# Rounding constants of a block quantisation in two PSUM banks, copied to SBUF by ScalarE for GpSimd's subtraction

## Chip, cores and metric

One core of a Trainium2 chip runs the whole program. The metric is the device time of one execution in microseconds, lower is better. The engines are named as in the profile: PE (TensorE), DVE (the Vector engine), ACT (ScalarE), POOL (GpSimd) and SP (SyncE, which only issues DMAs here).

## What is computed

Two transformer-like layers over x of shape (4, 1024, 256). Each branch is: layer norm with a modulation of scale and shift, the branch, a gated residual. Layer 0 has a dilated causal attention and a linear layer whose input and weight are quantised. Layer 1 has a Mamba block (a convolution, a selective state-space scan over time with 512 channels and 16 states) and a gated recurrence. What matters here is the quantisation of layer 0 and, as the load beside it, the scan of layer 1.

```python
def _mx_quantize(t, eps=1e-30):            # blocks of 32 along the features
    scales = max(max|block| / 7.5, eps)
    q = nearest value of the FP6 grid (2 exponent bits, 3 mantissa bits) to block / scale
...
xd = (xq * xs[..., None]).reshape(x2.shape)
out = xd @ wd.T + bias
...
def step(h, inp):                          # Mamba: one step in time
    h = a * h + bx
    y = einsum('bds,bs->bd', h, c)
```

The grid is reached by rounding in floating point. For a scaled value v the exponent bits of v are kept (a bitwise and with 0x7F800000), the result is raised to at least 1 and multiplied by 1.5 * 2^20. Adding this constant to v and subtracting it again rounds v to 3 mantissa bits.

## The kernel before

The tokens are cut into G = 8 halves of 512 tokens (two for each batch entry). For each half the front part (attention, quantised linear layer, convolution and projections: `pe_before`, `act_before`, `dve_before`, `pool_before`, named here "before(h)") runs beside the scan of the half in front of it, and the back part (`*_after`: output projection, gates) beside the scan of the next. The scan is the frame: 32 steps for each half, one step for each pair of channel groups and state, 256 steps in all. A step m is:

- ACT makes the decays (`act_decay`, L1186): two instructions ps<-arena 128x512, into a ring of three PSUM banks (0 to 2). They wait for the product of the step before.
- POOL makes the inputs (`pool_scan`, L1824): one instruction 128x1024, two steps ahead, in a ring of three.
- DVE runs two scans (`dve_scan`, L1606), then multiplies the states by C (the product, L1620, 128x1024 or twice 128x512), which frees the banks.
- PE adds the product to the sums y (`pe_scan`, L837, two matmuls, two records each, in banks 3 and 4).

All five queues are written out by hand and run in order. `in_time` merges the chains of the front and back parts into the scan: every piece of a chain has a due time in steps (`TIMES`, in quarters of a step), and it is issued on its engine ahead of the scan's part of the first quarter that reaches it. before(h) begins at step 32(h-1) - 5.25. Half 0 is done ahead of the scan, and halves 1 to 7 run beside it, so the stretch of this document occurs seven times.

The quantisation in before(h), h = 1 to 7, on 128 partitions x 1024 elements:

- DVE: largest magnitude of each block (L1237), scale (L1240), its reciprocal (L1243).
- POOL: input times the reciprocal, in place (L1738), then a bias into the residual (L1639, L1641).
- DVE: the bitwise and into `scr` (L1252, "the mask"), max and multiply on `scr` in place (L1255, "the multiply"), then, behind the product of step 12 of the half, `out = src + scr` (L1258, "the add"). All of `src`, `scr` and `out` are 1024-element pieces of the SBUF tensor `arena`.
- POOL: `out - scr` (L1743, "the subtraction") and times the scale (L1746), then two scan inputs (L1824), which are those of steps 15 and 16.
- PE transposes the result (L429), ACT copies it (L1024), PE multiplies by the weight (L581), ACT copies the result out (L1028), POOL adds it to the residual (L1645).

The semaphore `q_step` counts the nine steps of the quantisation. POOL's subtraction waits for its seventh, the add. The two PSUM banks X0 and X1 (5 and 6) serve the matmuls of the front part. Between the copies out of the attention's output projection (L1016) and the transposes (L429) nothing is in them. Half 0 and the weight are quantised by DVE alone (`shared=False`).

## Time and profile before

| what | value |
|---|---|
| median of 3 runs | 1396.28 us (1389.59 to 1400.68) |
| the profiled execution | 1395.78 us |
| its span, first to last instruction | 1394.5 us |
| busy: PE, DVE, ACT, POOL | 85%, 90%, 57%, 71% of the span |
| mean granted TensorE clock | 0.937 |

The profiled execution lies within 0.5 us of the median, and 1.3 us lie around its span. All durations below are from this one execution. Busy shares are means over stages of different kinds, so the stretch around the change is read by itself.

### The profile page before, as it was taken

The numbers are of one execution on the slowest core, as the hardware profiler recorded it, in microseconds if no ns is written. First come the engines' busy times: TensorE is split into PE (matmuls) and PEld (weight loads), VectorE is DVE, ScalarE is ACT, GpSimd is POOL, SyncE is SP. The second block draws the span as 40 slices with busy tenths as digits, with TensorE's granted clock in tenths as the row PEclk, the third lists the DMA queues.
The fourth block names the chain that finished last, engine by engine and source line by source line (L and its number), as shares of the span: only waits on it lengthen the run. The fifth ranks groups of instructions, "written<-read, shape, count | busy, mean of one in ns | idle before, by whom it ended". The sixth has DMA issues, their size and how long they took to land.

```text
span 1394.5 us, 12718 instructions
## 1 busy us (share of the span) xinstructions
PE 1190.2 (85%) x3576; PEld 654.7 (47%) x3576; DVE 1256.8 (90%) x1720; ACT 794.2 (57%) x1341; POOL 985.7 (71%) x521
## 2 busy tenths in 40 slices
PE   7757777798999979898989979898999979788895
PEld 5525332463446534573446533573446533343453
DVE  4667999899998999899998999899998999999976
ACT  3156454764676645765676645765676645744532
POOL 3207874788768895988768895988768895885842
PEclk9788979899999999999999999999999999899997
DMA  7203334432444336342444336342444334474711
GB/s 269 93 16 130 102 114 147 127 113 81 143 137 137 100 111 200 118 136 79 144 138 135 103 109 200 120 136 78 144 138 136 103 109 133 132 256 132 226 54 75
DMA packets 92023, 179.67 MB, mean 129 GB/s; under 512 B 10400, under 2 KB 15648, under 8 KB 91696
## 3 DMA queue, kind: packets, MB, share of 16 engines
q1 hardware_dynamic: 88928, 169.55, 37.8%
q10 hardware_dynamic: 3024, 9.31, 1.9%
q8 instruction: 28, 0.46, 0.1%
q14 instruction: 43, 0.35, 0.1%
HBM read 167.51 MB, written 11.31 MB: 128 GB/s over the span
## 4 chain that ended last, share of the span: by engine, by line
DVE 37%; PE 34%; ACT 15%; issue 11%; POOL 2%; DMA 1%; DVEq 0%; SPq 0%; POOLq 0%; ACTq 0%
DVE ps L1606 16%; PE ps L837 9%; DVE arena L1620 8%; PE ps L541 4%; DVE ps L1324 4%; ACT ps L1186 3%; PE ps L771 3%; PE ps L587 3%; PE ps L549 2%; ACT arena L861 2%; PE ps L581 2%; PE ps L573 2%; PE ps L676 2%; PE ps L557 2%; DVE stats_before L1218 1%
## 5 line engine op out<-in xcount | busy, mean ns | idle before, releaser
L1824 POOL TENSOR_TENSOR arena<-arena 128x1024 f32<-128x1024 f32 x255 | 604.9, 2387 | 204.8 <-DVE ps L1606 176.4
L1606 DVE TENSOR_TENSOR_SCAN ps<-ps,arena 128x512 f32<-128x512 f32 x512 | 622.0, 1247 | 52.2 <-ACT ps L1186 51.9
L837 PE MATMUL ps<-arena,identF 128*128 128x512 f32 x1024 | 504.9, 621 | 50.1 <-DVE arena L1620 45.0
L1186 ACT ACTIVATE ps<-arena,negA 128x512 f32<-128x512 f32 x512 | 332.7, 683 | 266.7 <-DVE arena L1620 265.7
L837 PEld LDWEIGHTS ps<-arena,identF 128*128 128x128 f32 x1024 | 195.7, 198 | 276.7 <-issue 196.9
L1620 DVE TENSOR_TENSOR arena<-ps,arena 128x1024 f32<-128x1024 f32 (+1 forms) x341 | 316.9, 950 | 6.8 <-PE ps L837 4.1
L1634 POOL TENSOR_TENSOR rnln<-vnln,consts 128x4 f32<-128x4 f32 x32 | 33.4, 1043 | 80.7 <-DVE vnln L1234 80.7
L852 ACT ACTIVATE arena<-arena,rnln 128x256 f32<-128x256 f32 x128 | 66.2, 589 | 41.0 <-POOL rnln L1636 41.0
L587 PE MATMUL ps<-arena,inw 128*128 128x512 f32 x128 | 72.1, 718 | 17.9 <-ACT arena L861 14.0
L668 PE MATMUL ps<-arena,inw 128*128 128x512 f32 x128 | 63.0, 615 | 13.9 <-DVE arena L1486 13.9
L1324 DVE SCALAR_TENSOR_TENSOR ps<-arena,vecs,ps 128x512 f32<-128x512 f32 x96 | 64.8, 749 | 6.6 <-ACT ps L964 6.6
L429 PE MATMUL ps<-identF,arena 128*128 128x128 f32 x248 | 39.2, 304 | 35.4 <-ACT arena L852 13.1
L1645 POOL TENSOR_TENSOR arena<-arena 128x512 f32<-128x512 f32 x42 | 53.1, 1274 | 22.3 <-ACT arena L1016 10.9
L861 ACT ACTIVATE arena<-ps,modT 128x512 f32<-128x512 f32 x45 | 53.9, 1264 | 18.6 <-PE ps L429 17.9
L429 PEld LDWEIGHTS ps<-identF,arena 128*128 128x128 f32 x248 | 32.2, 157 | 57.3 <-issue 24.4
L771 PEld LDWEIGHTS ps<-cpw,arena 128*128 128x128 f32 x224 | 54.7, 327 | 6.8 <-issue 5.3
L771 PE MATMUL ps<-cpw,arena 128*128 128x256 f32 x224 | 55.6, 403 | 0.0
L587 PEld LDWEIGHTS ps<-arena,inw 128*128 128x128 f32 x128 | 28.5, 228 | 55.2 <-issue 32.9
L541 PE MATMUL ps<-arena,wqT 128*128 128x128 f32 (+2 forms) x128 | 41.1, 472 | 9.7 <-ACT arena L861 9.7
L1119 ACT ACTIVATE arena<-ps,vecs 128x512 f32<-128x512 f32 x48 | 32.5, 678 | 27.2 <-PE ps L684 19.6
L668 PEld LDWEIGHTS ps<-arena,inw 128*128 128x128 f32 x128 | 23.1, 190 | 50.6 <-DVE arena L1486 27.9
L1758 POOL TENSOR_TENSOR arena<-arena 128x1024 f32<-128x1024 f32 x14 | 32.9, 2353 | 18.2 <-ACT arena L1068 18.2
(200 smaller groups left out, 1775.5 us busy)
## 6 DMA issues: line engine op xcount, KB each, us to landing
arena<-bc_scratch SPq DMA_DIRECT2D x519, 256.0 KB, 3.5
arena<-in_x SPq DMA_DIRECT2D x16, 256.0 KB, 4.6
arena<-in_x SPq DMA_DIRECT2D x8, 512.0 KB, 6.2
out_x<-arena SPq DMA_DIRECT2D x8, 512.0 KB, 2.7
xr_scratch<-arena SPq DMA_DIRECT2D x6, 512.0 KB, 4.4
px_scratch<-arena SPq DMA_DIRECT2D x6, 512.0 KB, 4.5
arena<-px_scratch ACTq DMA_DIRECT2D x6, 512.0 KB, 5.3
arena<-xr_scratch ACTq DMA_DIRECT2D x6, 512.0 KB, 6.0
```

The lines of the kernel that those rows point to most:

```text
L429: x = pe.transpose(ps[:, bank, j * P:(j + 1) * P], src[:, j, k * P:(k + 1) * P], identF[:])
L541: x = pe.matmul(ps[:, bank, cols[0]:cols[1]], w[:, h, k, :], hB1[:, k, 0:TH:TH // (cols[1] - cols[0])], start=(k == 0), stop=(k == KE - 1))
L587: x = pe.matmul(ps[:, bank, :], inw[:, k, kd * P:(kd + 1) * P], hB3[:, k, :], start=(k == 0), stop=(k == KE - 1))
L668: x = pe.matmul(ps[:, Y0, :], inw[:, k, DI + kd * P:DI + (kd + 1) * P], hB3[:, k, :], start=(k == 0), stop=(k == KE - 1))
L771: x = pe.matmul(ps[:, Y0, (j % 2) * E:(j % 2 + 1) * E], y2T[:, kd, j:TH:JH], cpw[:, kd, :], start=(kd == 0), stop=(kd == KD - 1))
L837: x = pe.matmul(ps[:, Y + q, :], identF[:], hc[:, m % 3, q, :], start=False, stop=(s == NS - 1), skip_group_check=True)
L861: act.activation(out, src, ACT.Identity, bias=modT[:, layer_col + k, b:b + 1], scale=modT[:, layer_col + 2 + k, b:b + 1]).then_inc(ln[site ...
L1186: act.activation(state_bank(n), dt[:, 2 * p + q, :], ACT.Exp, scale=negA[:, 2 * p + q, s:s + 1]).then_inc(S.decay, 1)
L1324: dve.scalar_tensor_tensor(x, xb[:, kd, tap:tap + TH], vec("conv", kd * TAPS + tap), x, ALU.mult, ALU.add).then_inc(S.conv, 1)
L1606: dve.tensor_tensor_scan(state_bank(n), state_bank(n), inp[:, m % 3, quarter, :], first, ALU.mult, ALU.add).then_inc(S.scan, 1)
L1620: x = dve.tensor_tensor(hc[:, m % 3, q:q + n, :], states, c_at[:, m % 3:m % 3 + 1, :].broadcast_to([P, n, TH]), ALU.mult)
L1824: pool.tensor_tensor(inp[:, m % 3, :, :], u[:, 2 * p:2 * p + 2, :], b_at[:, m % 3:m % 3 + 1, :].broadcast_to([P, 2, TH]), ALU.mult).then_i ...
```

## The change

In halves 1 to 7 the mask and the multiply write the PSUM banks X0 and X1 instead of `scr` in SBUF, and the add reads its constants from there. ACT gets a new instruction that copies both banks to `scr` once the add is done, and counts a new semaphore `q_scr`. POOL's subtraction waits for that instead of the add. The copy is due at 18.5 in both tables, `act_before` and `act_second` (the one for half 1). No other due time changes. Half 0 and the weight keep their constants in SBUF.

```diff
 "act_before": {
...
-        "op_ev": (13.25, 13.25), "hn2": (14.75, 14.75), "xdT": (19.5, 19.5), "ffn_ev": (20.75, 20.75),
+        "op_ev": (13.25, 13.25), "hn2": (14.75, 14.75), "q_scr": 18.5, "xdT": (19.5, 19.5), "ffn_ev": (20.75, 20.75),
...
@@ act_before(h)
+            yield t + T["q_scr"]
+            act.wait_ge(S.q_step, NQUANT * h + 7)
+            act.activation(scr.rearrange("p (q n) -> p q n", q=2), ps[:, X0:X0 + 2, :], ACT.Copy).then_inc(S.q_scr, 1)
             for k in range(KE):
                 yield t + T["xdT"][k]
                 act.wait_ge(S.xd_mm, 2 * h + k + 1)
...
@@ dve_quantise(src, out, n, scr_, step, at, times, shared=False)
+            src_, out_ = (x.rearrange("p (q n) b -> p q n b", q=2) if shared else x for x in (src, out))
...
             dve.wait_ge(step, at + 4)
-            dve.tensor_scalar(scr_.bitcast(I32), src.bitcast(I32), 0x7F800000, None, ALU.bitwise_and).then_inc(step, 1)
+            dve.tensor_scalar(scr_.bitcast(I32), src_.bitcast(I32), 0x7F800000, None, ALU.bitwise_and).then_inc(step, 1)
...
             dve.tensor_scalar(scr_, scr_, 1.0, 1.5 * 2 ** 20, ALU.max, ALU.mult).then_inc(step, 1)
...
-            dve.tensor_tensor(out, src, scr_, ALU.add).then_inc(step, 1)
+            dve.tensor_tensor(out_, src_, scr_, ALU.add).then_inc(step, 1)
...
@@ dve_before(h)
             dve.wait_ge(S.n2b, h + 1)
-            yield from dve_quantise(v32(K[0]), v32(K[2]), nblk, v32(scr), S.q_step, NQUANT * h,
+
+            grid = ps[:, X0:X0 + 2, :].rearrange("p q (n b) -> p q n b", b=BLOCK)
+            yield from dve_quantise(v32(K[0]), v32(K[2]), nblk, grid, S.q_step, NQUANT * h,
                                     [t + x for x in T["q_steps"]], True)
...
@@ pool_before(h)
             yield t + T["q_sub"]
-            pool.wait_ge(S.q_step, at + 7)
+            pool.wait_ge(S.q_scr, h)
             pool.tensor_tensor(out, out, v32(scr), ALU.subtract).then_inc(S.q_step, 1)
```


ScalarE's queue around the quantisation of half 2, before. L1186 is a decay, L1119 a gate's activation, L1024 the copies of the transposes, L1028 the copies out of the linear layer:

```order
L1119 ACTIVATE arena<-ps,vecs 128x512 [waits g_mm]
L1186 ACTIVATE ps<-arena,negA 128x512 [waits prod]
L1186 ACTIVATE ps<-arena,negA 128x512
L1186 ACTIVATE ps<-arena,negA 128x512 [waits prod]
L1186 ACTIVATE ps<-arena,negA 128x512
L1024 ACTIVATE arena<-ps 128x512 [waits xd_mm] x2
L1186 ACTIVATE ps<-arena,negA 128x512 [waits prod]
L1186 ACTIVATE ps<-arena,negA 128x512 [waits dt_add]
```

The same place with the change (L1189, L1122, L1027 and L1031 are the same instructions under new line numbers, L1023 is the copy):

```order
L1122 ACTIVATE arena<-ps,vecs 128x512 [waits g_mm]
L1189 ACTIVATE ps<-arena,negA 128x512 [waits prod]
L1189 ACTIVATE ps<-arena,negA 128x512
L1023 ACTIVATE arena<-ps 128x1024 [waits q_step]
L1189 ACTIVATE ps<-arena,negA 128x512 [waits prod]
L1189 ACTIVATE ps<-arena,negA 128x512
L1027 ACTIVATE arena<-ps 128x512 [waits xd_mm] x2
L1189 ACTIVATE ps<-arena,negA 128x512 [waits prod]
L1189 ACTIVATE ps<-arena,negA 128x512 [waits dt_add]
```

The copy stands behind the two decays that wait for the product of step 12, and ahead of the two that wait for the product of step 13.

GpSimd's queue at the subtraction of half 2, before (L1641 is the bias, L1824 a scan input, L1743 the subtraction):

```order
L1641 TENSOR_TENSOR arena<-arena,gbias 128x1024 [waits gbias]
L1824 TENSOR_TENSOR arena<-arena 128x1024 [waits scan,brow_in0]
L1824 TENSOR_TENSOR arena<-arena 128x1024 [waits scan,brow_in1]
L1743 TENSOR_TENSOR arena<-arena 128x1024 [waits q_step]
L1746 TENSOR_TENSOR arena<-arena,qsc 128x1024 [waits q_step]
L1824 TENSOR_TENSOR arena<-arena 128x1024 [waits scan,brow_in2]
L1824 TENSOR_TENSOR arena<-arena 128x1024 [waits scan,brow_in0,u]
```

And with the change (L1647, L1830, L1749 and L1752 are the same instructions):

```order
L1647 TENSOR_TENSOR arena<-arena,gbias 128x1024 [waits gbias]
L1830 TENSOR_TENSOR arena<-arena 128x1024 [waits scan,brow_in0]
L1830 TENSOR_TENSOR arena<-arena 128x1024 [waits scan,brow_in1]
L1749 TENSOR_TENSOR arena<-arena 128x1024 [waits q_scr]
L1752 TENSOR_TENSOR arena<-arena,qsc 128x1024 [waits q_step]
L1830 TENSOR_TENSOR arena<-arena 128x1024 [waits scan,brow_in2]
L1830 TENSOR_TENSOR arena<-arena 128x1024 [waits scan,brow_in0,u]
```

The order is the same; only the semaphore that the subtraction waits for is another. DVE's and PE's orders don't change, but DVE's mask now is `ps<-arena`, its multiply `ps<-ps` and its add `arena<-arena,ps`.

## Rows read from the trace of the kernel before

**Rows 1.** The page: busy time, and the chain that ended last
```profile
PE 1190.2 (85%) x3576; PEld 654.7 (47%) x3576; DVE 1256.8 (90%) x1720; ACT 794.2 (57%) x1341; POOL 985.7 (71%) x521
DVE 37%; PE 34%; ACT 15%; issue 11%; POOL 2%; DMA 1%; DVEq 0%; SPq 0%; POOLq 0%; ACTq 0%
```

**Rows 2.** Source lines, Vector engine: ns min/median/max, first and last start, forms
```profile
L1252 DVE TENSOR_SCALAR arena<-arena x9: 427/2286/2343, 30.0 to 1116.3; 128x1024 int32<-128x1024 int32 x8, 128x512 int32<-128x512 int32 x1
L1255 DVE TENSOR_SCALAR arena<-arena x9: 427/2716/2721, 30.4 to 1118.7; 128x1024 f32<-128x1024 f32 x8, 128x512 f32<-128x512 f32 x1
L1258 DVE TENSOR_TENSOR arena<-arena x9: 694/2170/2240, 30.9 to 1122.5; 128x1024 f32<-128x1024 f32 x8, 128x512 f32<-128x512 f32 x1
```

**Rows 3.** Groups by form: busy us, mean ns, idle before and its releaser
```profile
L1422 DVE TENSOR_SCALAR arena<-arena 128x1024 f32<-128x1024 f32 x1 | 0.7, 694 | 0.0
L1513 DVE TENSOR_TENSOR ps<-ps,bias_rows 128x1024 f32<-128x1024 f32 x1 | 1.2, 1233 | 0.7 <-issue 0.7
L1620 DVE TENSOR_TENSOR arena<-ps,arena 128x1024 f32<-128x1024 f32 x171 | 208.0, 1217 | 4.4 <-PE ps L837 2.6
L1157 ACT ACTIVATE arena<-arena 128x1024 f32<-128x1024 f32 x8 | 8.4, 1053 | 13.6 <-DVE arena L1566 6.9 <-DVE arena L1515 6.6
L1024 ACT ACTIVATE arena<-ps 128x512 f32<-128x512 f32 x14 | 7.7, 595 | 6.3 <-PE ps L429 6.3
```

**Rows 4.** Timeline, Vector engine, quantisation of half 6: start us, us, instruction [idle before]
```profile
959.65 2.29 DVE L1252 TENSOR_SCALAR arena<-arena 128x1024 int32<-128x1024 int32 x1
961.98 2.72 DVE L1255 TENSOR_SCALAR arena<-arena 128x1024 f32<-128x1024 f32 x1
964.62 1.27 DVE L1620 TENSOR_TENSOR arena<-ps,arena 128x512 f32<-128x512 f32 x2
965.82 2.17 DVE L1258 TENSOR_TENSOR arena<-arena 128x1024 f32<-128x1024 f32 x1
967.91 2.45 DVE L1606 TENSOR_TENSOR_SCAN ps<-ps,arena 128x512 f32<-128x512 f32 x2
...
975.18 2.46 DVE L1606 TENSOR_TENSOR_SCAN ps<-ps,arena 128x512 f32<-128x512 f32 x2
```

**Rows 5.** Timeline, GpSimd, the same stretch
```profile
961.35 5.56 POOL L1824 TENSOR_TENSOR arena<-arena 128x1024 f32<-128x1024 f32 x2
968.07 2.35 POOL L1743 TENSOR_TENSOR arena<-arena 128x1024 f32<-128x1024 f32 x1 [1.16 <-DVE arena L1258]
970.50 1.91 POOL L1746 TENSOR_TENSOR arena<-arena,qsc 128x1024 f32<-128x1024 f32 x1
972.37 4.69 POOL L1824 TENSOR_TENSOR arena<-arena 128x1024 f32<-128x1024 f32 x2
```

**Rows 6.** Timeline, ScalarE, the same stretch
```profile
965.93 1.30 ACT L1186 ACTIVATE ps<-arena,negA 128x512 f32<-128x512 f32 x2 [2.84 <-DVE arena L1620]
```

**Rows 7.** Timeline, TensorE, the same place in half 6 and in half 3
```profile
961.86 2.74 PE L837 MATMUL ps<-arena,identF 128*128 128x512 f32 x6
965.95 1.98 PE L837 MATMUL ps<-arena,identF 128*128 128x512 f32 x4 [1.35 <-DVE arena L1620]
...
494.65 2.47 PE L837 MATMUL ps<-arena,identF 128*128 128x512 f32 x4 [3.23 <-DVE arena L1620]
496.91 3.13 PE L676 MATMUL ps<-arena,gwf 128*128 128x512 f32 x4
```

**Rows 8.** Windows, half 3; after POOL busy: PEclk, DMA share, GB/s
```profile
496.00:500.00 4.00, 4.00 (x7) 1.66 (x6) 3.97 (x5) 0.00 (x0) 3.28 (x2) 0.57 0.46 132
```

**Rows 9.** Timeline, Vector engine, after the quantisation of half 3
```profile
509.27 1.23 DVE L1606 TENSOR_TENSOR_SCAN ps<-ps,arena 128x512 f32<-128x512 f32 x1 [0.65 <-ACT ps L1186]
```

**Rows 10.** Timeline, Vector engine and GpSimd, half 1
```profile
176.52 1.21 DVE L1258 TENSOR_TENSOR arena<-arena 128x1024 f32<-128x1024 f32 x1
191.79 1.23 DVE L1606 TENSOR_TENSOR_SCAN ps<-ps,arena 128x512 f32<-128x512 f32 x1 [2.06 <-ACT ps L1186]
...
177.81 2.35 POOL L1743 TENSOR_TENSOR arena<-arena 128x1024 f32<-128x1024 f32 x1 [2.96 <-DVE arena L1258]
```

More of the change, by code:

```diff
@@ L63 @@
         "k1": 8, "v0": 9.75, "exp1a": 9.75, "exp1b": 9.75, "att0": 11.25, "v1": 11.25, "att1": 12.25,
-        "op_ev": (12.75, 12.75), "hn2": (14.75, 14.75), "xdT": (19.5, 19.5), "ffn_ev": (21.25, 21.25),
+        "op_ev": (12.75, 12.75), "hn2": (14.75, 14.75), "q_scr": 18.5, "xdT": (19.5, 19.5), "ffn_ev": (21.25, 21.25),
         "hn3": (24, 24), "hB3": (24.5, 24.5), "xc_init": (25.5, 25.5, 27.5, 27.5),
@@ L114 @@
 ATTENTION = ["q_mm", "k_mm", "q_ev", "k_ev", "v_mm", "s_mm", "nmax", "e_ev", "rsum", "v_ev",
-             "att_mm", "att_ev", "gbias", "xbias", "op_mm", "op_tmp", "res0", "n2a", "n2b", "q_step", "xd_mm", "xdT",
+             "att_mm", "att_ev", "gbias", "xbias", "op_mm", "op_tmp", "res0", "n2a", "n2b", "q_step", "q_scr", "xd_mm", "xdT",
              "ffn_mm", "ffn_tmp", "res1"]
```

## Prediction

> **What bounds the kernel now.** I read the page first: DVE is busy for 90% of the span, PE for 85%, and the chain that ended last gives 37% to DVE and 34% to PE [rows 1]. These are means, so I went to the stretch of the change. The timeline of DVE there [rows 4] shows no idle time at all: mask, multiply, product, add and the scans follow each other from 959.65 to beyond 967.91 us. DVE sets the pace of this stretch. It repeats in halves 1 to 7.
>
> The reader is to look next at durations. The mask takes 2286 ns (median), the multiply 2716, the add 2170 [rows 2]. Others of the same size in SBUF are far shorter: a TENSOR_SCALAR of 128x1024 took 694 ns at the start of the program, where POOL had little to do, and in half 1, with POOL idle, the add itself took 1.21 us instead of 2.17 [rows 3, 10]. The timeline of POOL says why [rows 5]: it runs one instruction of 128x1024 after another, and where DVE's mask and multiply lie, its pair of scan inputs takes 5.56 us, though two of them took 4.69 a little later. So the two engines keep each other waiting, and DVE pays most. DVE's product, with one operand in PSUM and one in SBUF, takes 1217 ns on the mean of 171 although POOL is busy beside most of them [rows 3]. It doesn't wait.
>
> This is the lock that the Trainium skill describes, page "SBUF — State Buffer", section "Who interferes with whom": DVE and GpSimd share one pair of ports, a fast single-input instruction in SBUF or one with two SBUF inputs contends for it, and the later one waits out the other. By that rule all three instructions leave the contest, since none of them keeps all its tensors in SBUF or reads two from there. The rows above say the same of the product.
>
> **The change part by part.**
>
> DVE. Mask and multiply in PSUM are not in the trace. Nearest rows: an instruction that reads and writes 128x1024 in PSUM took 1233 ns, one from PSUM to SBUF 1217 [rows 3]. The fast SBUF form, 694 ns, is the lower end for each; the upper end is what they take now, 2.29 and 2.72, if the waiting stays. I take 1.22 and 1.25, since the 1233 ns row is nearest. The add becomes an instruction of the product's kind: 1.22. Sum 3.7 us against 2.29 + 2.72 + 2.17 = 7.2 us, so DVE has 3.5 us less to do in each half.
>
> A rule speaks against the change: the Trainium skill, page "VectorE: DVE Perf Modes", section "Why PSUM operands drop a tier", says that any PSUM operand takes fp32 down to one element a cycle. The undisturbed 694 against 1233 ns agree. By that rule alone the mask and multiply would lose 2 x 0.54 us and the seven halves 7.5 us.
>
> But undisturbed is not what these instructions are [rows 2], so I take the difference of the disturbed rows. How much of the 3.5 us arrives is decided by who is late next. I replay half 6 from 959.65 us:
>
> - mask to 960.9, multiply to 962.1, product to 963.3, add to 964.5. The product waits for sums of three steps earlier, which PE does ahead of the six records that it runs from 961.86 to 964.60 [rows 7], so it isn't held.
> - ACT's two decays, which now start at 965.93 behind the product [rows 6], start at 963.4 and end at 964.7 (1.30 us). The copy of 128x1024 follows. Its price: an SBUF copy of that size took 1053 ns, a PSUM copy of half of it 595 [rows 3], so between 1.05 and 2 x 0.595 = 1.19; I take 1.05, as the second half saves a start. It ends at 965.8. Behind it are the decays for the next step, which wait for a product at 968 anyway. ACT's 7 x 1.05 us cost nothing.
> - POOL: its pair of scan inputs starts at 961.35 and, no longer disturbed, takes 4.69 as the later pair did, to 966.05. The copy has ended by then, by 0.25 us. The subtraction starts at 966.1 instead of 968.07, the scaling ends at 966.1 + 2.35 + 0.08 + 1.91 = 970.4 and the next scan input at 972.8. These durations are those of rows 5. This input is the next to be late.
> - DVE: scans of step 13 to 966.9, product to 968.1, scans of 14 to 970.5, product to 971.7. The scans of step 15 want the input of 972.8 and wait about 1.1 us. Before they started at 975.18 [rows 4]. Gain 2.3 us, not 3.5: POOL takes the rest.
>
> What follows in that half (PE's transposes and the linear layer, ACT's copies, POOL's additions) comes 1.6 us or more earlier, since PE had idled 1.35 us for the product and was then busy without a gap [rows 7]. The scan has some slack against it in the even halves, so 2.3 us stay for halves 2, 4 and 6.
>
> In the odd halves PE idles longer, 3.23 us in half 3. Behind the idle time four records of the sums take 2.47 us instead of the 1.98 of half 6, and the next four, of a gate and of the same size, 3.13; the granted clock of 496 to 500 us is 0.57 of full speed, so part of it ran at 1.2 GHz and not 2.4 [rows 7, 8]. This makes the linear layer late, and DVE waits 0.65 us for ACT [rows 9] (three such waits: halves 3, 5 and 7). With the product 2.6 us earlier that idle time shrinks to about 0.7 us. Even if the clock still fell, PE would be 2.55 us ahead, so the wait goes: 2.3 + 0.65 = 2.95 us.
>
> Half 1: the add was undisturbed. POOL's subtraction started at 177.81 behind it [rows 10]. DVE's three instructions shrink by 2.29 + 2.72 + 1.21 - 3.7 = 2.5 us. The copy behind the add costs 1.05 and a hand-over of 0.1, so the subtraction comes 1.3 us earlier. DVE later waits 2.06 us for ACT [rows 10], which waits for the linear layer behind this subtraction, so 1.3 us is what is left. A little may come from PE's clock; I take 1.6.
>
> Sum: 1.6 + 3 x 2.3 + 3 x 2.95 = 17.3 us. From the profiled 1395.8 us that makes 1378.5 us, a gain of 1.24%. The median is only 0.5 us above the profiled time.
>
> **Rivals.**
>
> A. The gain is real on DVE but less of it arrives: the copy is later than I say, or the linear layer's chain sets the end of the stretch at its 1.6 us and then loses some more. For: POOL and PE are near full there, and the copy has only 0.25 us of room. Against: every engine's wait in the replay is for DVE or POOL, which both gain. With 1.3 us a half it is 7 x 1.3 = 9 us: 1387 us, within 1% of before.
>
> B. Slower. Mask and multiply still wait for POOL, because one side of the mask is in SBUF or because PSUM isn't what makes the product immune. Then the three keep their 7.2 us and the copy is added in front of POOL's subtraction, 1.15 us. DVE's slack at the scan input of step 15 is 975.18 less the end of that input, 972.37 + half of the pair's 4.69 = 974.72 [rows 4, 5], 0.46 us. So 0.7 us are lost in each even half, and in the odd ones and half 1, where the linear layer's chain already holds DVE, 1.15: 3 x 0.7 + 4 x 1.15 = 6.7 us, 1402.5 us. The point from which this decides: the subtraction starts later than now if the three take more than 968.07 - 959.65 - 1.2 (product) - 1.15 = 6.1 us. Against it stand the product's 171 undisturbed instances.
>
> C. The rule on tiers alone, the skill's page on the perf modes named above: PSUM costs its tier and the waiting was something else, which moving doesn't cure but which strikes only in SBUF's fast mode by chance of position. Worked out from rows: 7 x (2 x 0.54) = 7.5 us more on DVE, which is never idle there, 1403 us. I hold it for nearly excluded, since the three medians repeat in all halves [rows 2].
>
> D. More than forecast: PE keeps its clock in the odd halves and in half 1, and POOL, no longer disturbed, keeps ahead elsewhere too. All of DVE's 3.5 us in six halves and 3 in half 1 would be 24 us, 1372 us. POOL's chain in the replay speaks against it.
>
> **How the numbers follow.** Forecast 60%, A 27%, B 5%, C 2%, D 6%. The range holds the forecast, D and most of A: 1371 to 1389 us. A measurement of this kernel can tell about 1% from no change. The forecast, at 1.24%, lies close to that bound (1382.3 us from the median), so I give a quarter of its own chance to "within 1%". Faster by over 1%: 0.45 from the forecast, 0.06 from D and a little of A, 0.54. Slower by over 1% would take more than B: 0.03. The rest, 0.43, is within 1%.
>
> **What would show it.** In the changed profile the mask, multiply and add take 1.2 to 1.25 us each in halves 1 to 7 and still 694 ns or 1.2 us in half 0. POOL's pair of inputs beside them takes 4.7 us. The subtraction waits little or not at all for the copy in halves 2 to 7, and DVE has a wait of about 1 us for POOL before the scans of step 15. ACT's copy takes 1.05 us. PE idles under 1 us before the sums of step 12 in the odd halves, and the three waits of 0.65 us are gone. The forecast is wrong if mask or multiply stay above 2 us (B), if the subtraction waits long for ACT (A), or if DVE shows a new wait for ACT or PE later in each half.

## The result and the profile after

The changed kernel takes 1373.22 us (median of 4 runs, 1368.44 to 1373.75) against 1392.93 us of the kernel before (4 runs, 1389.06 to 1400.68): the ratio is 0.9856, with a 95% interval of 0.9828 to 0.9885. The change makes the kernel faster, by 1.4%. Its profiled execution took 1373.27 us with a span of 1372.0 us, where the one before had 1394.5 us: 22.5 us less. The medians differ by 19.7 us. The prediction had 17.3.

The page of the changed kernel, busy time and the chain that ended last, to be held against [rows 1]:

```profile
PE 1170.4 (85%) x3576; PEld 644.7 (47%) x3576; DVE 1231.8 (90%) x1720; ACT 800.5 (58%) x1348; POOL 979.0 (71%) x521
DVE 35%; PE 30%; ACT 15%; issue 11%; POOL 7%; DMA 1%; DVEq 0%; SPq 0%; POOLq 0%; ACTq 0%
```

DVE lost 25 us of busy time, close to 7 x 3.5. ACT gained 6.3, with seven copies of 1.0 in it. PE lost 19.8 us with the same number of instructions, at a mean granted clock of 0.952 instead of 0.937. POOL's share of the chain grew from 2 to 7%: it is late now where it wasn't. The three edited source lines and the copy, halves 1 to 7 (ns min/median/max, first and last start), against [rows 2]:

```profile
L1256 DVE TENSOR_SCALAR ps<-arena x7: 1195/1197/1202, 171.3 to 1095.9; 128x1024 int32<-128x1024 int32 x7
L1259 DVE TENSOR_SCALAR ps<-ps x7: 1232/1232/1233, 172.6 to 1097.2; 128x1024 f32<-128x1024 f32 x7
L1262 DVE TENSOR_TENSOR arena<-arena,ps x7: 1209/1210/1211, 174.9 to 1099.5; 128x1024 f32<-128x1024 f32 x7
...
L1023 ACT ACTIVATE arena<-ps x7: 999/1001/1003, 176.3 to 1100.9; 128x1024 f32<-128x1024 f32 x7
```

2286, 2716 and 2170 ns became 1197, 1232 and 1210, and minimum and maximum of each line lie within 7 ns of each other. That alone proves little, since the multiply before, which did wait, also stayed within 2.71 and 2.72 us in all seven halves. What shows that they no longer wait is that they keep these times beside a GpSimd that is busy, as the next views show.

The timeline of DVE in the quantisation of half 6, against [rows 4] (start us, us, instruction, [idle before and its releaser]):

```profile
943.44 1.20 DVE L1256 TENSOR_SCALAR ps<-arena 128x1024 int32<-128x1024 int32 x1
944.67 1.23 DVE L1259 TENSOR_SCALAR ps<-ps 128x1024 f32<-128x1024 f32 x1
...
947.01 1.21 DVE L1262 TENSOR_TENSOR arena<-arena,ps 128x1024 f32<-128x1024 f32 x1
948.13 2.46 DVE L1612 TENSOR_TENSOR_SCAN ps<-ps,arena 128x512 f32<-128x512 f32 x2
...
956.47 2.47 DVE L1612 TENSOR_TENSOR_SCAN ps<-ps,arena 128x512 f32<-128x512 f32 x2 [0.99 <-POOL arena L1830]
```

From the mask to the scans of step 15 it is 956.47 - 943.44 = 13.03 us; before it was 15.53. So 2.5 us arrive of the 3.5 that DVE saves, and the rest is the new wait in the last row. GpSimd in the same stretch, against [rows 5]:

```profile
942.83 2.35 POOL L1647 TENSOR_TENSOR arena<-arena,gbias 128x1024 f32<-128x1024 f32 x1
945.14 4.67 POOL L1830 TENSOR_TENSOR arena<-arena 128x1024 f32<-128x1024 f32 x2
949.77 2.36 POOL L1749 TENSOR_TENSOR arena<-arena 128x1024 f32<-128x1024 f32 x1
...
954.07 4.67 POOL L1830 TENSOR_TENSOR arena<-arena 128x1024 f32<-128x1024 f32 x2
```

The bias (first row) runs from before the mask's start to beyond its end, and the mask takes 1.20 us all the same. GpSimd is now without a gap: 4.67 for the pair instead of 5.56, the subtraction behind it without a wait, and half of the second pair ends at 956.4, just where DVE's scans start.

How the two engines met before can be read from the ends of their instructions. The bias of half 6 before was this row, which belongs ahead of those of [rows 5]:

```profile
959.04 2.35 POOL L1641 TENSOR_TENSOR arena<-arena,gbias 128x1024 f32<-128x1024 f32 x1
```

It ended at 961.39, and the mask that had started at 959.65 ended 0.55 us after it, at 961.94. The multiply ended at 964.70. The second scan input ended at 966.91, 2.21 us after the multiply, and if the first took as long behind the mask, the multiply ended 0.55 us after it too (an estimate: 961.94 + 2.21 = 964.15). The add, begun at 965.82, ended 1.08 us after the second input, at 967.99. So each engine waited for the other's instruction to end and then took nearly the time that it takes alone. The 0.55 us between the bias and the mask are there in all seven halves (0.54 to 0.55), the 1.08 us behind the pair in halves 2 to 7 (1.08 to 1.09). After the change each of the three takes its fixed time wherever POOL's instructions end.

The copy stands in ACT's timeline, against [rows 6]:

```profile
947.12 1.30 ACT L1189 ACTIVATE ps<-arena,negA 128x512 f32<-128x512 f32 x2 [0.54 <-DVE arena L1626]
948.37 1.00 ACT L1023 ACTIVATE arena<-ps 128x1024 f32<-128x1024 f32 x1
```

It ends at 949.37, 0.4 us before POOL can begin its subtraction. The view of waits has this one as new, over the whole program (us in total, times, longest):

```profile
DVE ps L1612 <- POOL arena L1830: 6.4, 7, 1.0
```

It comes seven times, once in each half from 1 to 7 (0.61 us in half 1, 0.88 to 1.01 in the others).

**Where 22.5 us went.** The start of the mask in each half cuts the program into periods. Worked out from the timelines (us):

```
                                   before    after     less
start to the mask of half 1        170.31   171.33     -1.0
half 1                             161.25   160.63      0.6
half 2                             156.61   154.06      2.6
half 3                             157.39   152.36      5.0
half 4                             156.94   153.66      3.3
half 5                             157.15   151.40      5.8
half 6                             156.64   152.49      4.2
mask of half 7 to the end          278.2    276.1       2.1
```

Halves 3, 5 and 6 give far more than the quantisation's 2.5 us (3.15 and 3.07 in halves 3 and 5, with the wait of 0.65 and 0.57 us that is gone there). Some 100 us behind the mask, in the attention of the next half, DVE waited for ACT for 1.9 to 2.0 us in all six of these periods. After the change this wait is there in halves 1, 2 and 4, and nearly gone in just 3, 5 and 6. Half 5 of the kernel before, timelines of TensorE and DVE:

```profile
895.38 0.77 PE L557 MATMUL ps<-arena 128*128 128x128 f32 x2 [2.25 <-ACT arena L985]
...
903.43 1.29 DVE L1606 TENSOR_TENSOR_SCAN ps<-ps,arena 128x512 f32<-128x512 f32 x1 [1.99 <-ACT ps L1186]
```

and its windows there (us, busy time of PE, PEld, DVE, ACT and POOL, then PEclk, DMA share, GB/s):

```profile
896.00:900.00 4.00, 4.00 (x17) 3.01 (x16) 4.00 (x6) 1.30 (x2) 3.92 (x3) 0.65 0.03 8
```

The same place after, the same views:

```profile
880.81 0.46 PE L557 MATMUL ps<-arena 128*128 128x128 f32 x2 [2.22 <-ACT arena L985]
...
887.21 1.29 DVE L1612 TENSOR_TENSOR_SCAN ps<-ps,arena 128x512 f32<-128x512 f32 x1 [0.34 <-ACT ps L1189]
```

```profile
880.00:884.00 4.00, 3.19 (x19) 2.54 (x20) 3.96 (x6) 1.97 (x4) 3.92 (x2) 1.00 0.02 4
```

TensorE has idled 2.2 us in both. Before, the granted clock then fell (0.65 of full speed over 4 us, so for most of them 1.2 GHz and not 2.4), two records took 0.77 us instead of 0.46, and everything behind was late. After, it stayed at 1.00, in this window and in the next. Nothing that the change edits lies there.

The higher clock isn't in this one profile alone. The mean granted clock of other runs is on record: 0.952 to 0.955 in the four runs of the changed kernel, 0.937 to 0.954 with a median of 0.948 in 27 runs of the kernel before. How the change would bring that is not shown.

### The profile page after: what moved, and what is told of

Same layout as the page of the kernel before. It is cut to its first block, busy times and chain, and to the rows that moved or that the text cites. A ratio compares the mean times of both kernels' runs of the same rounds, so it can differ in the third digit from the quotient of the medians.

```text
span 1372.0 us, 12725 instructions
## 1 busy us (share of the span) xinstructions
PE 1170.4 (85%) x3576; PEld 644.7 (47%) x3576; DVE 1231.8 (90%) x1720; ACT 800.5 (58%) x1348; POOL 979.0 (71%) x521
## 4 chain that ended last, share of the span: by engine, by line
DVE 35%; PE 30%; ACT 15%; issue 11%; POOL 7%; DMA 1%; DVEq 0%; SPq 0%; POOLq 0%; ACTq 0%
DVE ps L1612 16%; DVE arena L1626 8%; PE ps L837 7%; PE ps L541 4%; DVE ps L1328 4%; POOL arena L1830 3%; ACT ps L1189 3%; PE ps L771 3%; PE ps L549 2%; PE ps L587 2%; ACT arena L861 2%; PE ps L573 2%; DVE stats_before L1221 1%; PE ps L557 1%; ACT arena L852 1%
## 5 line engine op out<-in xcount | busy, mean ns | idle before, releaser
L1830 POOL TENSOR_TENSOR arena<-arena 128x1024 f32<-128x1024 f32 x255 | 598.6, 2362 | 200.0 <-DVE ps L1612 172.0
L837 PE MATMUL ps<-arena,identF 128*128 128x512 f32 x1024 | 496.0, 612 | 36.0 <-DVE arena L1626 30.2
L1189 ACT ACTIVATE ps<-arena,negA 128x512 f32<-128x512 f32 x512 | 332.8, 684 | 237.5 <-DVE arena L1626 236.6
L587 PE MATMUL ps<-arena,inw 128*128 128x512 f32 x128 | 68.0, 682 | 19.7 <-ACT arena L861 14.9
L668 PE MATMUL ps<-arena,inw 128*128 128x512 f32 x128 | 63.6, 620 | 14.2 <-DVE arena L1492 14.2
L1122 ACT ACTIVATE arena<-ps,vecs 128x512 f32<-128x512 f32 x48 | 32.6, 679 | 25.9 <-PE ps L684 18.4
```

What stands on the lines that cost most here:

```text
L587: x = pe.matmul(ps[:, bank, :], inw[:, k, kd * P:(kd + 1) * P], hB3[:, k, :], start=(k == 0), stop=(k == KE - 1))
L668: x = pe.matmul(ps[:, Y0, :], inw[:, k, DI + kd * P:DI + (kd + 1) * P], hB3[:, k, :], start=(k == 0), stop=(k == KE - 1))
L837: x = pe.matmul(ps[:, Y + q, :], identF[:], hc[:, m % 3, q, :], start=False, stop=(s == NS - 1), skip_group_check=True)
L1189: act.activation(state_bank(n), dt[:, 2 * p + q, :], ACT.Exp, scale=negA[:, 2 * p + q, s:s + 1]).then_inc(S.decay, 1)
L1830: pool.tensor_tensor(inp[:, m % 3, :, :], u[:, 2 * p:2 * p + 2, :], b_at[:, m % 3:m % 3 + 1, :].broadcast_to([P, 2, TH]), ALU.mult).then_i ...
```

## The experiments

Three of them take the change apart, four ask what can be had on top, and the last four are about the clock.

**handover.** The kernel before, with a pass of ACT between the add and the subtraction, and nothing in PSUM.

```diff
+            act.wait_ge(S.q_step, NQUANT * h + 7)
+            act.activation(scr, scr, ACT.Copy).then_inc(S.q_scr, 1)
...
-            pool.wait_ge(S.q_step, at + 7)
+            pool.wait_ge(S.q_scr, h)
```

> The kernel before with only the hand-over of the change: constants stay in SBUF, ScalarE copies scr onto itself behind the add (1.05 us), and GpSimd's subtraction waits for that copy. My theory (the port pair is what the change removes, the copy itself costs where GpSimd had been waiting for the add): the subtraction starts 1.15 us later in each of seven halves, DVE loses 0.7 us in the even and 1.15 us in the other halves, 6.7 us or 0.5% slower than before (ratio 1.005), mask and multiply stay at 2.29 and 2.72 us. Rival (the slack in the scan covers it): ratio 1.000.

Measured: ratio 1.0040 (1.0027 to 1.0053). Timelines of DVE and GpSimd in its half 6:

```profile
960.53 2.30 DVE L1256 TENSOR_SCALAR arena<-arena 128x1024 int32<-128x1024 int32 x1
962.86 2.72 DVE L1259 TENSOR_SCALAR arena<-arena 128x1024 f32<-128x1024 f32 x1
...
966.70 2.17 DVE L1262 TENSOR_TENSOR arena<-arena 128x1024 f32<-128x1024 f32 x1
...
962.23 5.56 POOL L1829 TENSOR_TENSOR arena<-arena 128x1024 f32<-128x1024 f32 x2
970.04 2.35 POOL L1748 TENSOR_TENSOR arena<-arena 128x1024 f32<-128x1024 f32 x1 [2.25 <-ACT arena L1023]
```

The interval leaves out the rival's 1.000: the hand-over alone costs 0.4%. DVE's three stay where they were and the subtraction waits 2.25 us instead of 1.16, and in this half DVE reaches the scans of step 15 0.7 us later, as expected. So the gain doesn't come from the hand-over. This run is also close to what rival B would have been (its copy reads SBUF, not PSUM): 0.4% of its 1391.8 us before are 5.6 us for a copy behind a quantisation as slow as ever, where the prediction had 6.7.

**mult_sbuf.** The mask in PSUM, the multiply back to SBUF, the add of two SBUF tensors; no copy.

```diff
-            dve.tensor_scalar(scr_, scr_, 1.0, 1.5 * 2 ** 20, ALU.max, ALU.mult).then_inc(step, 1)
+            dve.tensor_scalar(con, scr_, 1.0, 1.5 * 2 ** 20, ALU.max, ALU.mult).then_inc(step, 1)
...
-            dve.tensor_tensor(out_, src_, scr_, ALU.add).then_inc(step, 1)
+            dve.tensor_tensor(out_, src_, con, ALU.add).then_inc(step, 1)
```

> Only the mask goes to PSUM; the multiply reads PSUM and writes scr in SBUF, the add reads two SBUF tensors, and there is no copy by ScalarE. Theory (an instruction waits for GpSimd if it reads two SBUF tensors or is in the fast SBUF form): mask 1.2 us, multiply 1.2 us, add 1.6 to 2.2 us, and the add in turn delays GpSimd's pair of scan inputs by 1.2 us (5.9 us instead of 4.7), so DVE reaches the scans of step 15 about 1.1 us later than with the whole change: 7 to 8 us slower than it, a ratio to before of about 0.991. Rival (only the two single-input instructions matter): the time of the whole change, ratio 0.985, or better since the copy is gone.

Measured: 0.9905 (0.9881 to 0.9929). DVE and GpSimd, half 6:

```profile
951.09 1.20 DVE L1253 TENSOR_SCALAR ps<-arena 128x1024 int32<-128x1024 int32 x1
952.32 1.22 DVE L1257 TENSOR_SCALAR arena<-ps 128x1024 f32<-128x1024 f32 x1
...
954.65 1.57 DVE L1260 TENSOR_TENSOR arena<-arena 128x1024 f32<-128x1024 f32 x1
...
965.09 1.29 DVE L1610 TENSOR_TENSOR_SCAN ps<-ps,arena 128x512 f32<-128x512 f32 x1 [1.59 <-POOL arena L1828]
...
952.79 5.64 POOL L1828 TENSOR_TENSOR arena<-arena 128x1024 f32<-128x1024 f32 x2
```

The add with both operands in SBUF is the only one of the three that still takes longer: 1.57 us, and POOL's pair 5.64 instead of 4.67. The ends fit again. The first input of the pair, with its 2.35 us, ends at 955.14, the add 1.08 us later at 956.22, and the second input 2.21 us after that. DVE loses 0.36 us by that, POOL 0.97, and POOL is the late one. Mask and multiply alone, without any copy, bring two thirds of the gain (0.95 of 1.44%). The interval leaves out the rival's 0.985.

**mask_sbuf.** The mask in SBUF, the multiply from SBUF to PSUM, add and copy as changed.

```diff
-            dve.tensor_scalar(scr_.bitcast(I32), src_.bitcast(I32), 0x7F800000, None, ALU.bitwise_and).then_inc(step, 1)
+            dve.tensor_scalar(exps.bitcast(I32), src_.bitcast(I32), 0x7F800000, None, ALU.bitwise_and).then_inc(step, 1)
...
-            dve.tensor_scalar(scr_, scr_, 1.0, 1.5 * 2 ** 20, ALU.max, ALU.mult).then_inc(step, 1)
+            dve.tensor_scalar(scr_, exps, 1.0, 1.5 * 2 ** 20, ALU.max, ALU.mult).then_inc(step, 1)
```

> Only the mask stays in SBUF; multiply SBUF to PSUM, add from PSUM, copy by ScalarE. Theory: mask 2.3 us as before, multiply and add 1.2 us each, GpSimd's pair of scan inputs 5.4 us instead of 4.7 because the mask holds the ports once; DVE had 1.0 us of slack before the scans of step 15, so only GpSimd's 0.65 us count: 4.6 us slower than the whole change, ratio to before 0.989. Rival (DVE's own time is what counts): 1.1 us in each half, 7.7 us slower than the whole change, ratio 0.991. If the multiply still waits with its input in SBUF (2.7 us), the theory on the ports is wrong.

Measured: 0.9891 (0.9860 to 0.9922). DVE and GpSimd, half 6:

```profile
950.53 2.29 DVE L1257 TENSOR_SCALAR arena<-arena 128x1024 int32<-128x1024 int32 x1
952.86 1.23 DVE L1260 TENSOR_SCALAR ps<-arena 128x1024 f32<-128x1024 f32 x1
...
964.32 1.29 DVE L1613 TENSOR_TENSOR_SCAN ps<-ps,arena 128x512 f32<-128x512 f32 x1 [0.65 <-POOL arena L1831]
...
952.23 5.12 POOL L1831 TENSOR_TENSOR arena<-arena 128x1024 f32<-128x1024 f32 x2
957.63 2.35 POOL L1750 TENSOR_TENSOR arena<-arena 128x1024 f32<-128x1024 f32 x1 [0.27 <-ACT arena L1023]
```

The mask that stays in SBUF costs 2.29 us as before; the multiply is cured although it reads SBUF. So it doesn't take a move out of SBUF altogether: one side in PSUM is enough, whichever it is (1.20 and 1.23 with the output there, 1.22 with the input, 1.23 with both). POOL's pair was lengthened less, to 5.12, than the 5.4 expected: it waits only for the 0.5 us by which the mask outlasts the bias. The interval holds both the theory's 0.989 and the rival's 0.991, so the time doesn't tell whether GpSimd's or DVE's own lateness counts. In this profile DVE reaches the scans of step 15 0.76 us later than with the change, where the theory had 0.65 and the rival 1.1.

**early_bias.** The change, and two things on top: ACT copies as soon as the multiply is done, beside the product, so that the add waits for it; and POOL adds the bias to the residual ahead of the scaling.

```diff
-            act.wait_ge(S.q_step, NQUANT * h + 7)
+            act.wait_ge(S.q_step, NQUANT * h + 6)
...
+            if shared:
+                dve.wait_ge(S.q_scr, at // NQUANT)
             dve.tensor_tensor(out_, src_, scr_, ALU.add).then_inc(step, 1)
...
             yield t + T["q_scale"]
+            pool_bias_to_residual(GB0, 1, 2 * h + 2, xrow)
             src, out, at = v32(K[0]), v32(K[2]), NQUANT * h
...
-            yield t + T["gb_bias"]
-            pool_bias_to_residual(GB0, 1, 2 * h + 2, xrow)
...
-            pool.wait_ge(S.q_scr, h)
+            pool.wait_ge(S.q_step, at + 7)
```

(The copy's due time becomes 17.75 in both tables.)

> The whole change and two things more: ScalarE copies the constants while DVE runs the product (behind the multiply, not behind the add; the add waits for the copy so that the two never read the banks at once), and GpSimd does its bias (3.1 us) ahead of the scaling, where it waits for the reciprocal. Theory (after the change GpSimd's chain up to the scan input of step 15 is late by 1.0 us): the subtraction starts about 1.1 us earlier, the wait of DVE for that input goes, but the mask starts 0.4 us later: about 0.7 us gained in each half, 5 us faster than the whole change, ratio to before 0.982. Rival (that wait is covered by later waits): the time of the whole change, 0.9856.

Measured: 1366.95 us (1362.27 to 1370.72), ratio 0.9818 (0.9787 to 0.9849). ACT, DVE and GpSimd, half 6:

```profile
937.85 1.02 ACT L1023 ACTIVATE arena<-ps 128x1024 f32<-128x1024 f32 x1 [3.67 <-DVE ps L1259]
...
947.38 1.28 DVE L1614 TENSOR_TENSOR_SCAN ps<-ps,arena 128x512 f32<-128x512 f32 x1
...
940.27 2.35 POOL L1750 TENSOR_TENSOR arena<-arena 128x1024 f32<-128x1024 f32 x1 [0.36 <-DVE arena L1264]
```

The wait of the scans for POOL is gone, and from the mask (935.32) to them it is 12.06 us: the whole 3.5 us of DVE arrive. The expectation had 0.7 us for each half. Another 1.0 us in each of seven halves would be 7 us; its median lies 6 us below that of the change. It beats the kernel before clearly, and the changed one probably: the two intervals of the ratio overlap by 0.2 points. Which of the two edits does it? The next two runs take them apart.

**early_copy** has only the earlier copy, **bias_first** only the earlier bias.

> The whole change with only the copy moved ahead: behind the multiply, while DVE runs the product; the bias stays where it was. Theory (in halves 2 to 7 GpSimd's own queue, not the copy, decides when the subtraction starts): nothing in halves 2 to 7, 1.2 us in half 1, where the subtraction did wait for the copy (1.9 us): ratio to before 0.985. Rival (the copy is what held the subtraction): 5 us, 0.982.

> The whole change with only GpSimd's bias moved ahead of the scaling; the copy stays behind the add. Theory: the subtraction then waits for the copy, which ends at about the time at which it started before (0.05 us later), so nothing is gained: ratio to before 0.986, and the subtraction waits 1.0 to 1.5 us for ScalarE. Rival (the bias alone brings what both edits together brought): 0.982.

Measured: 0.9851 (0.9799 to 0.9904) and 0.9853 (0.9798 to 0.9907), each as the change itself. Both intervals also hold the rivals' 0.982, so the times alone don't decide; the rows do. GpSimd and DVE, half 6 of early_copy:

```profile
949.31 4.67 POOL L1832 TENSOR_TENSOR arena<-arena 128x1024 f32<-128x1024 f32 x2
953.93 2.36 POOL L1751 TENSOR_TENSOR arena<-arena 128x1024 f32<-128x1024 f32 x1
...
960.63 2.47 DVE L1614 TENSOR_TENSOR_SCAN ps<-ps,arena 128x512 f32<-128x512 f32 x2 [0.90 <-POOL arena L1832]
```

and of bias_first:

```profile
949.26 2.35 POOL L1748 TENSOR_TENSOR arena<-arena 128x1024 f32<-128x1024 f32 x1 [1.44 <-ACT arena L1023]
...
955.96 2.47 DVE L1612 TENSOR_TENSOR_SCAN ps<-ps,arena 128x512 f32<-128x512 f32 x2 [0.66 <-POOL arena L1829]
```

Each edit removes one of two limits that lie close together. With the early copy alone POOL's own queue is full up to the subtraction, and DVE waits 0.90 us for it as ever. With the early bias alone POOL is there in time and then waits 1.44 us for the copy, and DVE waits 0.66 us. Only both together let DVE go through. In half 1 the subtraction of early_copy comes 1.1 us sooner behind the mask than with the change (4.93 for 6.01 us), where 1.2 was expected.

**before_bias.** The kernel before with the bias ahead of the scaling, for whether that order is worth anything without PSUM.

> The kernel before with only the bias moved ahead of the scaling. Theory: the constants in SBUF still wait for GpSimd's scan inputs, mask and multiply take 2.3 to 3 us each, the add is undisturbed (1.2 us), and the scans behind start 0.4 us later than before: ratio 1.000 to 1.002. Rival (GpSimd's order was the fault, not the place of the constants): 0.996 or less, with mask and multiply under 1 us.

Measured: 1.0019 (0.9990 to 1.0048), nothing. DVE and GpSimd, half 6:

```profile
955.05 5.09 POOL L1823 TENSOR_TENSOR arena<-arena 128x1024 f32<-128x1024 f32 x2
...
955.12 2.82 DVE L1252 TENSOR_SCALAR arena<-arena 128x1024 int32<-128x1024 int32 x1
957.98 2.71 DVE L1255 TENSOR_SCALAR arena<-arena 128x1024 f32<-128x1024 f32 x1
...
961.81 1.21 DVE L1258 TENSOR_TENSOR arena<-arena 128x1024 f32<-128x1024 f32 x1
...
963.10 2.35 POOL L1742 TENSOR_TENSOR arena<-arena 128x1024 f32<-128x1024 f32 x1 [2.96 <-DVE arena L1258]
```

POOL is now idle during the add, which takes 1.21 us as it did in half 1 [rows 10], in place of 2.17. So the 0.96 us more were POOL's doing. But the mask takes 0.5 more: the waiting has moved. It now starts just behind a scan input and outlasts it by 0.55 us (955.05 + 2.34 against 957.94), and the multiply outlasts the second input by the same 0.55 (960.14 against 960.69).

This profiled execution has a surprise: not one of the six waits of 1.9 us in the attention is in it, and from the mask of half 1 to that of half 7 it takes 937.0 us, where the kernel before takes 946.0. That would be 1.5 us for each wait, if nothing else made it. The bias stands elsewhere in this kernel, and two new waits for ACT, of 1.78 and 1.52 us, have come in halves 2 and 3 behind the quantisation. But the medians of ten and thirteen runs show no gain from the order, and the profiled run was the fastest of its ten.

**before_delay**, **after_delay**, **before_again** and **after_again** are for these waits. The delayed kernels have three more additions on DVE at the start of the program, whose results are overwritten; the others are the two kernels as they were.

```diff
             dve.wait_ge(S.xin, 32)
+            for n in 'fic':
+                dve.tensor_tensor(gate_flat[n], att_flat, att_flat, ALU.add)
             dve_stats("ln1", xin, 0)
```

> The kernel before with three additions of 1.2 us put in front of DVE's first instruction (their results are not used), so that all of the program starts 3.7 us later or less. It tests where the part of the gain that the replay lacks comes from: in the kernel before, DVE waits 1.9 us for ScalarE in the attention of six halves, because the matmuls behind a 2.2 us idle time of TensorE run at the lower clock; in the changed kernel three of these six waits are gone although TensorE idles as long. Theory (chance of position in time): the span grows by up to 3.7 us, and the number of such waits comes out under six here too, with no edit near them. Rival (the waits go because of the change): six waits again.

> The kernel before once more, unchanged, for a second profiled execution. If the clock behind the same 2.2 us idle of TensorE depends on the place in time of the stretch, this execution shows VectorE's waits of about 1.9 us for ScalarE's L1186/L1189 in five or six of the six places again, and a span of 1393 to 1396 us. If it differs from execution to execution, their number is another one (0 to 4), and the span is shorter by about 1 us or more for each that is missing (1387 to 1392 us).

> The changed kernel once more, unchanged. If the place in time decides, three of the six waits of about 1.9 us are there again, at the same three places (about 274, 430 and 736 us), and the span is 1371 to 1373.5 us. If it differs from execution to execution, their number or their places are others and the span lies anywhere from 1368 to 1378 us. The stretch from the mask to the scans of step 15 takes 13.05 us in either case.

> The changed kernel with three additions of about 1.2 us at VectorE's start, which set everything behind them some 3.5 us or more later. If the place in time decides, the waits of about 1.9 us are at other places or in another number than in the changed kernel, and the span grows by anything but the delay. If nothing but the work decides, the same three are there and the span grows by 3.5 to 6 us, to 1375.5 to 1378.

Measured, one execution of each, with the numbers of the others beside them (us; the waits are those of about 1.9 us, 1.6 to 2.0 in these profiles, out of six):

```
                 first scan   mask 1 to mask 7   waits   span
before             109.68          946.0           6     1394.5
before_again       108.70          946.2           6     1392.6
before_delay       115.45          942.0           5     1394.1
handover           112.44          944.1           2     1395.4
before_bias        111.41          937.0           0     1387.8
after              110.81          924.6           3     1372.0
after_again        117.06          923.5           3     1376.4
after_delay        112.51          927.9           4     1377.1
```

The kernel before repeated itself, six waits in the same six periods, as its first expectation had it, though the span came 0.4 us under the range given. The changed kernel repeated only their number: in halves 1, 3 and 6 instead of 1, 2 and 4, as the other alternative had it. Its quantisation repeated to the hundredth, 13.03 us from the mask to the scans. So neither theory holds for both kernels. The waits differ between executions of one and the same kernel, and the later start of after_again may be why, or not. The span of before_delay didn't grow, though up to 3.7 us were expected. The three delaying additions took one wait away in one kernel and added one in the other, but they can't part place from chance: they moved the first scan by 5.8 and 1.7 us, and without any edit after_again moved it by 6.25. The span of after_delay grew by 5.1 us, inside the range that was given for unchanged waits, and the waits changed. The table leaves out five more executions with the new quantisation, whole or in part: mult_sbuf, mask_sbuf and early_bias have two such waits each, early_copy three, bias_first four, one of them 3.25 us long. What sets whether the clock falls behind the same 2.2 us of idle time stays open.

after_again shows the same at another place. Its first scan comes 6.25 us later than in the first execution, with the same instructions in front of it. TensorE there, first execution:

```profile
80.50 8.79 PE L587 MATMUL ps<-arena,inw 128*128 128x512 f32 x16 [1.43 <-DVE arena L1299]
92.61 1.10 PE L531 MATMUL ps<-arena 128*128 128x512 f32 x2 [3.32 <-DVE arena L1334]
```

and in after_again:

```profile
82.62 10.01 PE L587 MATMUL ps<-arena,inw 128*128 128x512 f32 x16 [1.43 <-DVE arena L1299]
95.94 2.05 PE L531 MATMUL ps<-arena 128*128 128x512 f32 x2 [3.32 <-DVE arena L1334]
```

The idle times are equal to the hundredth, the records are not: 8.79 or 10.01 us, 1.10 or 2.05. The granted clock was 1.00 from 92 to 96 us in the first and 0.66 from 94 to 98 us in the second; in the four microseconds in front of these it was 1.00 in both.

## Why the prediction was right, and where it was off

**The cause.** Right. Mask, multiply and add fell to 1.197, 1.232 and 1.210 us, 3.64 in all for the 3.7 of the sum, and handover, mult_sbuf and mask_sbuf show that it is the place of the tensors and not the hand-over that does it. The rule of the Trainium skill, page "SBUF — State Buffer", section "Who interferes with whom", by which a fast single-input instruction in SBUF and one with two SBUF inputs contend with GpSimd, agrees with each of the three: mult_sbuf's add, with two inputs in SBUF, is the only one of its instructions that still waits. The other rule of the Trainium skill, page "VectorE: DVE Perf Modes", section "Why PSUM operands drop a tier", by which a PSUM operand takes fp32 down to one element a cycle, agrees too (694 ns in SBUF undisturbed, 1232 in PSUM). It doesn't decide here, since before the change the mask and the multiply never had their 694 ns in halves 1 to 7. Rival C falls by that, and B by 3.64 us against its point of decision at 6.1.

**The replay of the even halves.** Right in each step. The copy has 0.4 us of room (predicted 0.25), POOL's pair takes 4.67 (4.69), the subtraction doesn't wait, and DVE waits 0.99 us for the scan input of step 15 (about 1.1). The copy took 1.00 us instead of 1.05, and the gain is 2.5 us instead of 2.3.

**The odd halves.** The three waits are gone, as forecast. Only that of half 3 was 0.65 us; those of halves 5 and 7 were 0.57, so the prediction's term was 0.16 us too large in all. Odd and even is also the pattern of one execution: in before_again DVE has this wait in half 3 and none in halves 5 and 7, where TensorE idles 1.5 us, and it waits 0.98 and 0.66 us in half 6, behind 3.05 us of idle time. In the changed kernel, ahead of the sums of step 12, TensorE idles 0.72 us in half 5 and 0.57 in half 7, in half 3 not at all (about 0.7).

**Half 1.** Too high: 1.6 us, of which 0.6 arrived. The subtraction's 1.3 us did come: relative to the mask, it and the linear layer start 1.5 us earlier than before. The timeline of TensorE there, before:

```profile
184.94 5.60 PE L581 MATMUL ps<-ffnT,arena 128*128 128x256 f32 x16 [0.78 <-ACT arena L1024]
```

and with the change, with DVE's wait behind it:

```profile
184.48 6.28 PE L581 MATMUL ps<-ffnT,arena 128*128 128x256 f32 x16 [0.78 <-ACT arena L1027]
...
192.01 1.23 DVE L1612 TENSOR_TENSOR_SCAN ps<-ps,arena 128x512 f32<-128x512 f32 x1 [3.18 <-ACT ps L1189]
```

The same sixteen records take 0.68 us longer at a clock that stays low longer (0.79 from 188 to 192 us; 0.90 in the same window before, and 0.50 from 184 to 188 us in both). "A little may come from PE's clock" had the wrong sign here: DVE's wait for ACT grew from 2.06 to 3.18 us. In after_again it is 2.63, and half 1 takes 160.17 us, 1.1 less than before, so this too differs between executions.

**What the sum hadn't got.** By the periods the quantisation's own gain in halves 2 to 6 is 5 x 2.5 + 0.65 + 0.57 = 13.7 us, where the prediction had 12.8. The three missing waits give 1.9 us in half 3, 2.7 in 5 and 1.7 in 6, together 6.2, if all that these halves gained beyond the quantisation is put down to them. Then 0.8 us are left, nearly all in half 4, that I can't name, and against them stand -1.0 for half 1, -0.85 in half 7 (2.1 for 2.95) and -1.0 ahead of the first mask. 17.3 + 0.9 + 6.2 + 0.8 - 1.0 - 0.85 - 1.0 = 22.35 us of the 22.5.

So the term that was missing is TensorE's clock in the attention, 100 us behind the edit. It isn't the reason for which rival D gave 24 us and 1372 us (POOL keeping ahead): POOL's wait is there, and that the measured 1373.2 us lies next to D's time is coincidence. Whether the changed kernel has fewer of these waits because of the change can't be settled by so few executions. The changed kernel and its delayed twin had 3, 3 and 4 of six, the kernel before and its delayed twin 6, 6 and 5, but handover and before_bias, with the old quantisation, 2 and 0, and the five other kernels with the new quantisation, whole or in part, 2, 2, 2, 3 and 4. The medians' gain, 19.7 us, lies between the sum and the profile's difference, as it should if part of that is luck of one execution. Of the 5.3 us between the forecast of 1378.5 and the measured median, 2.4 are this larger gain. The other 2.9 are no gain: the forecast started from the profiled 1395.8 us, and the kernel before then measured 1392.9 beside the changed one.

The range was held by 2.2 us at its lower end. Worked with six waits at the 1.5 us of before_bias, 9 us (an estimate), it should have reached further down. Rival D's 24 us also took 3 us in half 1, where the prediction's own sum has DVE shrink by only 2.5.

## What to carry to other kernels

Where a DVE instruction takes two to four times what its twin takes elsewhere in the same trace, and GpSimd is busy beside it, compare the durations by where the tensors lie before counting elements: here one operand in PSUM, on either side, saved about half of it (2.29 to 1.20 us, 2.72 to 1.22 or 1.23), although the undisturbed SBUF form, 0.69, is the faster one. Compare also where the instructions of the two engines end: a fixed distance, half after half, says who waited for whom. Then look who is late next and how closely: a POOL queue and a copy on ACT held the last 1 us together, and only both edits at once (early_bias) brought it. And read a gain of one per cent from several executions: thirteen runs of the unedited kernel before, beside early_copy, lie between 1387.75 and 1401.91 us, and two profiles of the changed one differ by 4.4 us of span.

## What was unexpected of the hardware

- The granted clock of TensorE behind an idle time isn't a function of that idle time. Behind 2.2 us it fell in some executions and places and not in others (two records 0.77 or 0.46 us), and behind 3.32 us the same two records took 1.10 or 2.05 in two executions of one kernel.
- The collision of DVE with GpSimd isn't shared evenly. A pair of POOL's instructions grows from 4.67 to 5.56 us beside a mask and a multiply that lose 1.6 and 2.0 us against their fast SBUF form, and to 5.64 beside a single add that loses only 0.36. The rows above say why: whoever is running goes to its end. An add that comes late in a scan input waits only for the rest of it, and the next input then waits for nearly all of the add.
- ACT's copy from PSUM, 1.00 us for 128x1024, is a little quicker than one in SBUF of the same size, 1.05 [rows 3], and 1.05 in handover too.
